# Attention inner cycle in another order: scores, values, then row maxima, with PSUM banks handed out one by one

## The reference

```python
h = _layernorm(x, ln1_g, ln1_b)
q = (h @ wq + bq).reshape(B, S, N_HEADS, dk)
k = (h @ wk + bk).reshape(B, S, N_HEADS, dk)
v = (h @ wv + bv).reshape(B, S, N_HEADS, dk)
scores = jnp.einsum('bqhd,bkhd->bhqk', q, k) / np.sqrt(dk).astype(np.float32)
attn = jax.nn.softmax(scores, axis=-1)
ctx = jnp.einsum('bhqk,bkhd->bqhd', attn, v).reshape(B, S, D)
x = x + ctx @ wo + bo
```

## Time and profile before

| | us |
|---|---|
| Median of 3 runs | 2846.17 |
| Lowest and highest | 2843.82, 2851.62 |
| The profiled execution, its own time | 2817.32 |
| Its span in the trace | 2815.6 |
| Attention, from the first max job to the last score matmul | 1245.7 to 2411.5 |

### The profile page before, as it was taken

One profiled execution on the slowest core, in us unless ns is written; L12 is line 12 of the kernel. 1 busy time (PEld: TensorE's weight loads), 2 busy tenths in 40 slices (PEclk: granted clock), 3 DMA queues, 4 the chain that ended last, 5 costly groups with the idle time before them and its releaser, 6 DMA issues. The chain is left out here.

```text
span 2815.6 us, 54580 instructions
## 1 busy us (share of the span) xinstructions
PE 2480.4 (88%) x20934; PEld 1926.7 (68%) x20934; DVE 2019.2 (72%) x2975; ACT 1576.9 (56%) x2658; POOL 1288.6 (46%) x749
## 2 busy tenths in 40 slices
PE   4889939999969998758999999999999999358995
PEld 3668829999968887735666666666666665148995
DVE  5775558888868866647777777778777775437885
ACT  4554426777744543315666666666666666226772
POOL 0001011222224302335888888888888888403331
PEclk9999959999989999967999999999999999658997
DMA  9986335666747754342000000130000000126674
GB/s 399 361 328 230 97 116 197 235 235 235 227 157 231 236 176 128 105 129 74 10 16 17 9 17 11 34 70 9 17 14 12 17 9 7 49 77 227 231 235 161
DMA packets 110400, 361.81 MB, mean 129 GB/s; under 512 B 21888, under 2 KB 48896, under 8 KB 92416
## 3 DMA queue, kind: packets, MB, share of 16 engines
q1 hardware_dynamic: 89152, 295.43, 30.7%
q0 software_dynamic: 18464, 55.59, 6.4%
q10 hardware_dynamic: 2592, 8.16, 0.7%
HBM read 314.30 MB, written 44.83 MB: 128 GB/s over the span
## 5 line engine op out<-in xcount | busy, mean ns | idle before, releaser
L1365 POOL TENSOR_TENSOR at_pool_sum<-at_pool_sum,at_probs 128x1024 f32<-128x1024 f32 x364 | 865.8, 2379 | 101.0 <-ACT at_probs L1491 60.4
L1520 DVE TENSOR_REDUCE at_part_max<-ps_x 128x2 f32<-128x1024 f32 x624 | 734.2, 1220 | 228.5 <-PE ps_x L1421 228.5
L1491 ACT ACTIVATE at_probs<-ps_s 128x512 f32<-128x512 f32 x1352 | 698.2, 604 | 325.3 <-PE ps_s L1380 302.6
L1380 PE MATMUL ps_s<-at_qst,at_kst 97*128 97x256 f32 x2704 | 518.3, 311 | 4.8 <-ACT at_probs L1491 4.0
L1380 PEld LDWEIGHTS ps_s<-at_qst,at_kst 97*128 97x128 f32 x2704 | 369.5, 190 | 218.3 <-ACT at_probs L1491 124.4
L1397 PE MATMUL ps_oz<-at_probs,k_xhat 128*32 128x256 f32 (+1 forms) x5408 | 392.3, 387 | 0.0
L577 PE MATMUL ps_acc<-adj_hi,y_hi 128*128 128x512 f32 (+1 forms) x728 | 290.2, 399 | 92.3 <-DVE adj_lo L643 61.9
L643 DVE TENSOR_TENSOR adj_lo<-adj_raw,adj_hi 128x1024 fp32r<-128x1024 f32 (+1 forms) x182 | 217.5, 1197 | 165.0 <-ACT adj_hi L419 162.8
L579 PE MATMUL ps_acc<-adj_hi,y_lo 128*128 128x512 f32 (+1 forms) x728 | 278.3, 382 | 0.0
L578 PE MATMUL ps_acc<-adj_lo,y_hi 128*128 128x512 f32 (+1 forms) x728 | 278.2, 382 | 0.0
L1025 ACT ACTIVATE ex_hid<-ps_ex_h,ex_b 128x256 f32<-128x256 f32 x432 | 197.2, 475 | 129.4 <-PE ps_ex_h L966 117.7
(11 more groups left out here) (227 smaller groups left out, 4021.0 us busy)
## 6 DMA issues: line engine op xcount, KB each, us to landing
ex_w<-w SPq DMA_DIRECT2D x108, 1024.0 KB, 7.6
adj_raw<-adjT SPq DMA_DIRECT2D x156, 512.0 KB, 4.6
k_xhat<-adj SPq DMA_DIRECT2D x26, 1664.0 KB, 7.5
at_qst<-qk_parts SPq DMA_DIRECT2D x78, 128.0 KB, 2.6
results<-ex_res POOLq DMA_DIRECT2D x34, 256.0 KB, 3.3
ex_b<-b SPq DMA_DIRECT2D x54, 128.0 KB, 2.3
adj_raw<-adjT_tail SPq DMA_DIRECT2D x26, 256.0 KB, 2.7
qk_parts<-qk_hi POOLq DMA_DIRECT2D x26, 256.0 KB, 2.8
```

Source lines behind the costliest of these rows:

```text
L1365: pool.tensor_tensor(pool_sum[:, g % 2], pool_sum[:, g % 2], probs[:, tile % RING], ALU.add).then_inc(pool_added, 1)
L1380: last = pe.matmul(ps_s[:, unit % S_BANKS, hh, :], kst[:, 2 * j + hh, k * P:(k + 1) * P], qst[:, g % 2, 2 * j + hh, :], start=True, stop=True)
L1491: act.activation(probs[:, tile % RING, 2 * j:2 * j + 2], ps_s[:, unit % S_BANKS], ACT.Exp, scale=scale).then_inc(taken, 1)
L1520: dve.tensor_reduce(part_max[:, g % 2, heads, qt, kc], ps_x[:, pair, :], AX.X, ALU.max).then_inc(x_free, 1)
```

## The change

PE's order in a cycle becomes a, b, c, d, values, and then the jobs. In c12 the output product goes ahead of the two max jobs, on PE and on DVE. The seven banks of scores and maxima become one tensor, and a plan made before the kernel is built gives each user a bank and what it has to wait for. Three banks are a ring for a, b, c, the row and the output product, which now uses one bank instead of two. Four banks go to the jobs; unit d gets the first of them, the one whose reduction ended first in the cycle before. DVE reduces each bank of a job by itself, so one reduction over 1024 elements becomes two over 512, and `x_free` counts banks.

```diff
     for cycle in range(-MAX_AHEAD, BLOCKS * CYCLES + OUT_AT + 1):
         now = []
+        g, c = divmod(cycle, CYCLES)
+        if c == OUT_AT and g >= 1:
+            now.append(("out", g - 1, 0, 0, 0))
         ahead, j = divmod(cycle + MAX_AHEAD, CYCLES)
         if ahead < BLOCKS:
             now += [(kind, ahead, qt, hp, kc) for kind, qt, hp, kc in full[2 * j:2 * j + 2]]
-        g, c = divmod(cycle, CYCLES)
-        if c == OUT_AT and g >= 1:
-            now.append(("out", g - 1, 0, 0, 0))
...
+X_PAIRS, S_RING = 2, 3
+def score_parts(c):
+    return [(2 * c, 0), (2 * c, 1), (2 * c + 1, 0), (2 * c + 1, 1)]
...
+def bank_plan(jobs, freed, tile_unit, row_unit):
+    unit_bank, job_banks, unit_waits, job_waits, holder = {}, {}, {}, {}, {}
+    ring = itertools.cycle(range(2 * X_PAIRS, 2 * X_PAIRS + S_RING))
+    order = list(range(2 * X_PAIRS))
+    def waits_for(banks):
+        waits = {}
+        for b in banks:
+            if b in holder:
+                kind, count = holder[b]
+                waits[kind] = max(waits.get(kind, 0), count)
+        return waits
+    def give_unit(unit, bank):
+        unit_bank[unit], unit_waits[unit] = bank, waits_for([bank])
+        holder[bank] = ("unit", unit + 1)
+    def give_job(u, banks):
+        job_banks[u], job_waits[u] = banks, waits_for(banks)
+        for n, b in enumerate(banks):
+            holder[b] = ("job", freed[u] + n + 1)
+    for cycle in sorted(jobs):
+        g, c = divmod(cycle, CYCLES)
+        if 0 <= g < BLOCKS:
+            for k, j in score_parts(c):
+                give_unit(tile_unit[g * NT + k] + j, order[0] if (k, j) == (2 * c + 1, 1) else next(ring))
+            order = [order[1], order[2], order[0], order[3]]
+        reductions = 0
+        for job in jobs[cycle]:
+            if job[1] in ("max", "tail"):
+                give_job(job[0], order[reductions:reductions + 2])
+                reductions += 2
+            else:
+                give_job(job[0], [next(ring)])
+        if c == ROW_AT and 0 <= g + 1 < BLOCKS:
+            for half in range(2):
+                give_unit(row_unit[g + 1] + half, next(ring))
...
             def run(job):
                 u, kind, g, qt, hp, kc = job
-                pair = u % 2 * 2
-                if u >= 2:
-                    pe.wait_ge(x_free, u - 1)
+                banks = job_banks[u]
+                bank_free(job_waits[u])
...
                         pe.wait_ge(taken, row_unit[g] + 2)
-                    scores(g, 2 * c, (0, 1))
-                    scores(g, 2 * c + 1, (0,))
-                for job in jobs[cycle]:
-                    if job[1] != "out":
-                        run(job)
-                if 0 <= g < BLOCKS:
-                    scores(g, 2 * c + 1, (1,))
+                    scores(g, score_parts(c))
                 if g >= 0 and c:
                     if g < BLOCKS:
                         values(g, 2 * c - 2)
...
                 for job in jobs[cycle]:
-                    if job[1] == "out":
-                        run(job)
+                    run(job)
                 if c == ROW_AT and 0 <= g + 1 < BLOCKS:
                     row(g + 1)
...
-                    dve.tensor_reduce(part_max[:, g % 2, heads, qt, kc], ps_x[:, pair, :], AX.X, ALU.max).then_inc(x_free, 1)
+                    for hh in range(2):
+                        dve.tensor_reduce(part_max[:, g % 2, 2 * hp + hh, qt, kc:kc + 1], ps_x[:, banks[hh], :], AX.X, ALU.max).then_inc(x_free, 1)
```

More of the change, by code:

```diff
@@ L1256, in score_units, with freed_counts @@
     return tile_unit, row_unit
+X_PAIRS, S_RING = 2, 3
+def score_parts(c):
+    return [(2 * c, 0), (2 * c, 1), (2 * c + 1, 0), (2 * c + 1, 1)]
+def freed_counts(flat):
+    counts, total = {}, 0
+    for u, kind, *_ in flat:
+        counts[u] = total
+        total += 2 if kind in ("max", "tail") else 1
+    return counts, total
+def bank_plan(jobs, freed, tile_unit, row_unit):
[32 more added lines that the diff above has]
+                give_unit(row_unit[g + 1] + half, next(ring))
+    return unit_bank, unit_waits, job_banks, job_waits
 def attend(nc, m, t, s):
@@ L1369, in _, with bank_free, scores @@
         def _(pe):
-            def scores(g, k, halves):
+            def bank_free(waits):
+                if "unit" in waits:
+                    pe.wait_ge(taken, waits["unit"])
+                if "job" in waits:
+                    pe.wait_ge(x_free, waits["job"])
+            def scores(g, parts):
                 hg = g // NCH
[L1372 to L1375, removed]
+                for k, j in parts:
+                    for n, (start, _) in enumerate(K_PIECES):
+                        if k == start and g % NCH == 0 and j == 0:
+                            pe.wait_ge(k_loaded[n], 48 * (hg + 1))
                     unit = tile_unit[g * NT + k] + j
-                    if unit >= S_BANKS:
-                        pe.wait_ge(taken, unit - S_BANKS + 1)
+                    bank_free(unit_waits[unit])
                     for hh in range(2):
-                        last = pe.matmul(ps_s[:, unit % S_BANKS, hh, :], kst[:, 2 * j + hh, k * P:(k + 1) * P],
+                        last = pe.matmul(ps_s[:, unit_bank[unit], hh, :], kst[:, 2 * j + hh, k * P:(k + 1) * P],
                                          qst[:, g % 2, 2 * j + hh, :], start=True, stop=True)
@@ L1420, in run @@
                         at = slice((2 * hp + hh) * DK, (2 * hp + hh + 1) * DK)
-                        last = pe.matmul(ps_x[:, pair + hh, :], queries[at, g % 2, qt * P:(qt + 1) * P],
+                        last = pe.matmul(ps_x[:, banks[hh], :], queries[at, g % 2, qt * P:(qt + 1) * P],
                                          keys[at, g // NCH, kc * KEYS:(kc + 1) * KEYS], start=True, stop=True)
@@ L1426, in run @@
                             at = slice((2 * hp + hh) * DK, (2 * hp + hh + 1) * DK)
-                            last = pe.matmul(ps_x[:, pair + hh, q * CHUNK:q * CHUNK + NP - kc * KEYS], queries[at, g % 2, q * P:(q + 1) * P],
+                            last = pe.matmul(ps_x[:, banks[hh], q * CHUNK:q * CHUNK + NP - kc * KEYS], queries[at, g % 2, q * P:(q + 1) * P],
                                              keys[at, g // NCH, kc * KEYS:NP], start=True, stop=True)
@@ L1433, in run @@
                     for q in range(QT):
-                        last = pe.matmul(ps_x[:, pair + q, 0:D], cx[:, q * P:(q + 1) * P], wo[:, g // NCH, :], start=True, stop=True)
+                        last = pe.matmul(ps_x[:, banks[0], q * D:(q + 1) * D], cx[:, q * P:(q + 1) * P], wo[:, g // NCH, :], start=True, stop=True)
                 last.then_inc(x_made, 1)
@@ L1490, in exponentials @@
                     act.wait_ge(scored, unit + 1)
-                    act.activation(probs[:, tile % RING, 2 * j:2 * j + 2], ps_s[:, unit % S_BANKS], ACT.Exp,
+                    act.activation(probs[:, tile % RING, 2 * j:2 * j + 2], ps_s[:, unit_bank[unit]], ACT.Exp,
                                    scale=scale).then_inc(taken, 1)
```

27 lines of the change are left out of this document (14 added, 13 removed).

## The result

| | before | after |
|---|---|---|
| Median, us | 2843.27 (20 runs) | 2858.04 (20 runs) |
| Lowest and highest, us | 2836.60, 2854.09 | 2847.10, 2866.01 |
| Ratio of after to before, 95% interval | | 1.0046 (1.0034 to 1.0058) |

The change makes the kernel 0.46% slower, which is 13 us; the two medians themselves differ by 14.8. The forecast was 0.7%, 19 us.

The account below looks back on a forecast made before the run. PE's own order was taken as the bound; the terms sum to +0.81 us per block, +19.4 over 24 blocks, less 1 at the end and up to 2 more at the start: +19 us, 2865 us; range +9 to +40 us (70%).

Parts of the forecast that it names:

- The loop: c1 to c10: scores a, four Exps, job 2, next scores make every cycle 3.16 us; +0.75 us per block.
- One sign: List of waits: job 2's load would show as PEld of the max jobs on ACT, some 0.15 to 0.6 each.
- The list of waits: Profile before: ACT's 302.6 us wait for PE's scores is the longest entry by far, so PE's order sets the pace.
- c11: Cycle 11, where the row stands behind job 2: 3.91 us instead of 3.81, +0.10; the other end gives -0.01.
- c12: Cycle 12, with the output product ahead of the jobs: next scores at 4.29 us instead of 4.50, -0.21.
- c0: Cycle 0, where unit d waits for DVE's first half until 1.33: 4.50 us instead of 4.33, +0.17.
- DVE's halves: Max reductions over 512 elements: each lasts 0.69 us, they follow at about 0.60, hidden while a half stays under 0.70.
- The ends: Run-in 0 to +2 us, first block zero, last 15 cycles -1 us because POOL fills them, bounded by -5.
- The faster kernel: Rival: the wait for d's Exp does not decide; -2.0 us a block, -49 us, 2797 us; 12%.
- the balance: Rival: gain and loss cancel, with a loop of 3.05 to 3.12 or lower ends together; within 8 us of 2846; 10%.
- DVE as the bound: Rival: halves follow at 0.80 instead of 0.60; +3 us a block, +75 us on top, 2940 us; 5%.
- the clock rival: Rival: the granted clock falls as PE rests 0.58 in share-free cycles; time above 2900 us; 3%.

Follow-up runs that it names:

- e2: Changed kernel with a small ACT copy that nothing reads added behind the Exp of unit a in every cycle; ratio 1.0234 to the kernel before.
- e3: Kernel before with the same small ACT copy as e2 behind the Exp of unit a; ratio 1.0004 to the kernel before.
- e8: Changed kernel with max reductions over 256 of each bank's 512 elements, a probe; ratio 1.0008 to the kernel before.
- e1: Changed kernel with ACT taking unit d before c, so job 2 waits for the third Exp instead of the fourth; ratio 0.9997 to the kernel before.
- e4: Kernel before with each max job reduced by two DVE instructions over 512 elements instead of one over 1024; ratio 1.0045.
- e6: Changed kernel with the output product of c12 behind the two max jobs again, on PE and DVE; ratio 1.0235 to the kernel before.
- e5: Kernel before with the order alone (a, b, c, d, values, jobs), output product last, banks and whole reductions as before; ratio 1.0428.
- e7: Kernel of e1 with max reductions over 256 of each bank's 512 elements, a probe; ratio 0.9759 to the kernel before.
- e9: Kernel of e1 with PE's output product of c12 between scores and values; ratio 0.9958 to the kernel before.

## Why the prediction was right

**The loop.** Its four links are all there: as medians 0.60 to 0.62, 2.06, 0.05, and 0.42 to 0.45 (forecast 0.61, 2.07, 0.05, 0.43). c1 to c10 take 31.60 as forecast, +0.75 a block. e2 against e3 and e8 show that it is this loop and not DVE, and e1 that job 2's wait for the fourth Exp closes it. The 0.14 by which unit d waits for its bank in c1 came too (0.85 instead of 0.71), hidden as forecast. One sign came only in part: the waits show ACT in front of job 2 in the share-free cycles (0.25 to 0.39) and not in the share cycles, where the delay of 0.15 is inside the length of the jobs' loads. The rule of the Trainium skill, "Perfetto Trace Analysis", section "Optimizing Scalar/DVE Operations", says that splitting the instructions of an engine which is not saturated but causes bubbles elsewhere may finish work sooner. It gave nothing in e4: the halves alone, with the old order, made the three cycles longer in which DVE was waited for, by 0.13 each, since there both banks of a job come free only after the second half. In the changed kernel the first bank comes free after 0.68 instead of 1.22, and that is the bank that unit d borrows; what the change would cost with whole reductions no run shows. By that rule alone the kernel would have become faster; it became slower.

**The list of waits.** ACT's 302.6 us for PE is its longest entry, but not by far: DVE's wait for PE stands next with 214.4. Both name PE, so the conclusion holds.

**The small terms.** The sum per block was +0.61, not +0.81, and three terms erred.

- c11: -0.10 instead of +0.10. Its step from job 2 to the row, 0.43, was right; the step "0.75 from its first load to the next scores" was the one that failed. From the row's first load to the scores it takes 0.54 behind a job, and the eight loads last 0.42 where they lasted 0.64 behind values:

```profile
1773.35 0.34 PEld L1488 LDWEIGHTS ps_x<-at_keys,at_queries 32*128 32x128 f32 x4 [0.41 <-issue]
1773.93 0.42 PEld L1512 LDWEIGHTS ps_x<-k_ident_b,at_maxima 128*1 128x1 bf16 x8 [0.24 <-issue]
1774.47 0.30 PEld L1448 LDWEIGHTS ps_x<-at_qst,at_kst 97*128 97x128 f32 x2
```

- c12: +0.12 instead of -0.21. The product starts at 3.12 (forecast 3.11), but I took its 0.75 from a row where scores followed; jobs follow after 1.06 (1777.59 to 1778.65).
- c0: -0.15 instead of +0.17. DVE's halves start at 4.90 of c12 (forecast 4.89), and unit d loads at 5.63. But c12 ended 0.33 later than forecast, and the same moment was 1.01 of c0 instead of 1.33:

```profile
1777.59 0.73 PEld L1501 LDWEIGHTS ps_x<-at_wo,at_cx 128*128 128x128 f32 x4 [0.41 <-ACT at_probs L1550]
1778.65 0.19 PEld L1488 LDWEIGHTS ps_x<-at_keys,at_queries 32*128 32x128 f32 x4 [0.33 <-issue]
1778.76 0.69 DVE L1590 TENSOR_TENSOR k_x<-ps_x,k_x 128x512 f32<-128x512 f32 x1 [2.39 <-PE ps_x L1501]
1779.09 0.78 PEld L1448 LDWEIGHTS ps_x<-at_qst,at_kst 97*128 97x128 f32 x6 [0.25 <-issue]
1779.37 2.47 DVE L1580 TENSOR_REDUCE at_part_max<-ps_x 128x1 f32<-128x512 f32 x4
1780.10 0.30 PEld L1448 LDWEIGHTS ps_x<-at_qst,at_kst 97*128 97x128 f32 x2 [0.24 <-DVE at_part_max L1580]
```

The errors of c12 and c0 are one error of 0.33, counted once too low and once too high, so it costs the sum nothing; what is left of 0.20 a block is c11's, 4.8 us over 24 blocks. That c0 took back what c12 had too much is no luck: unit d of c0 loads when DVE's first half has ended, however long c12 lasts, and that moment the prediction had right.

**DVE's halves** last 0.68 (forecast 0.69) and follow at 0.60 (four in 2.48).

**The ends.** The run-in grew by 2.1 us (forecast 0 to 2). The first block, counted as zero, is 2.2 us shorter: the granted clock of 0.50, with which the stage begins, ended 9.2 us after the first scores instead of 14.6. By an estimate from these numbers, 5.4 us less at half the clock are worth 2.7 us, and without them the block grows by 0.5 like the others. Why the clock rose earlier no run shows. In the last block POOL's last addition starts 40.18 us after the first scores against 40.16, so POOL does hold it; what follows ends 1.2 us later, where I had forecast -1. The granted clock differs there too, which the prediction left out: it fell to 0.50 at 41.2 us of the last block instead of 48.0, so that 8.7 us of the stage's end ran at the lower level instead of 0.7. How much of the 1.2 us is its doing no run separates. Together: 2.1 + 11.6 (the 25 blocks up to the last) + 1.2 = 14.9, the growth of the stage. The windows behind POOL's last addition, before the stage's end, first of before and then of after:

```profile
2412.40:2420.40 8.00, 4.52 (x52) 2.53 (x48) 2.53 (x9) 0.60 (x1) 3.15 (x3) 1.00 0.01 2
2436.40:2445.00 8.60, 3.13 (x12) 1.37 (x12) 2.47 (x9) 0.60 (x1) 2.00 (x2) 0.50 0.00 0
```

That the first block's -2.2 and the last block's +2.2 against its forecast cancel is luck.

**The range.** The prediction gives two: +9 to +40 us on 2846 is 2855 to 2886, and its range in us begins at 2847. The growth of 13 to 15 us lies in both, below the middle.

**The rivals.** The faster kernel, the balance, and DVE as the bound did not come, and neither did cycles that alternate. In the changed kernel the clock stayed at 1.00 from 9.2 us behind the first scores to the last block, with waits of 0.14 to 0.57 us for the fourth Exp in c1 to c10. e6 shows that the clock rival was no idle thought: behind rests of 1.85 us in one piece it fell in 14 blocks of 23.

**What each part of the change did.** The order by itself costs 125.7 us of stage (e5), since d waits bare for the Exp of a and the output product for DVE. The lent bank, with the halves that free it early, and the output product's new place take back all but 14.9. The gain that the order promises PE, 0.2 a cycle, exists (3.01 in e7's share cycles against 3.21), but a loop through ACT, and behind it one through DVE, lie above it.

## What to carry to other kernels

When a buffer is lent from one user to another, draw the loop that it closes: from the start of the cycle through the engine that empties it, to the instruction that waits for it, and on to whatever is queued behind that instruction. If the sum of the links is longer than the cycle, it becomes the cycle, however idle the engines are. Ask then which link can be shortened for nothing: here the order of two Exps gave the change's whole loss back. To tell whether an engine is on such a loop, add a small instruction to it in both kernels; full price in one and none in the other is an answer that no busy share gives. And price the steps between kinds of matmul by what stands on both sides of them.

## What the runs showed of the hardware that was not expected

- The four loads of the output product took 0.75 us up to the next loads when scores followed (and 0.76 in e6), and 1.06 when jobs or values followed (after and e9). The eight loads of the row took 0.75 up to the next scores behind values and 0.54 behind jobs.
- In e6 each of 23 blocks has one rest of PE's loads of about 1.85 us. Behind it the granted clock fell to the lower level for 3.41 us in 14 blocks (0.54 over 3.74 us in the one shown), which cost c0 1.6 us, and stayed at 1.00 in the other 9.
